# Sturm sweeps as two interleaved chains of 64 steps, and two edits inside the Householder steps, in a two-layer graph network kernel on one core

## The reference, cut to what matters

```
deg    = sum(A, 0) + sum(A, 1) - diagonal(A)
L_norm = d^-1/2 (diag(deg) - A) d^-1/2
_, U   = eigh(L_norm)                       # all 256 eigenvectors
agg    = einsum('mn,bnd->bmd', U.T, h);  o = relu(agg @ W1 + b1) @ W2 + b2
x      = x + einsum('nm,bmd->bnd', U, o)
# second block: two graph convolutions with adj, then LSTMs over windows of 1, 2, 3 and 4 nodes
```

## Time and profile before

| what | us |
|---|---|
| median of three runs | 1768.78 |
| the profiled execution, its own time | 1770.09 |
| span of the profile (first to last instruction) | 1768.2 |
| wide Householder steps (20.0 to 473.8) | 453.8 |
| narrow Householder steps (473.8 to 786.2) | 312.4 |
| first sweep, 64 values (796.4 to 898.8) | 102.4 |
| second sweep, 128 values (912.1 to 1039.4) | 127.3 |
| third sweep, 64 values (1046.1 to 1147.7) | 101.6 |
| everything behind it (1147.7 to 1768.2) | 620.5 |

### The profile page before, as it was taken

The page is one execution under the profiler, slowest core; times in us unless marked ns, Lnnn a source line. Parts: engine busy times, 40 slices in busy tenths (PEclk is TensorE's granted clock), DMA queues, the critical chain, the costliest instruction groups (busy, mean ns, idle before and its releaser), DMA issues.

```text
span 1768.2 us, 25450 instructions
## 1 busy us (share of the span) xinstructions
PE 1292.7 (73%) x5951; PEld 1067.5 (60%) x5951; DVE 1324.6 (75%) x6292; ACT 611.8 (35%) x2145; POOL 391.3 (22%) x2101
## 2 busy tenths in 40 slices
PE   7999999999866677752434323342978999999998
PEld 5777888888745555541222211241757668989897
DVE  7898988888888888888979988897572235555555
ACT  2222222222334442221112111230213367777776
POOL 4333333433455555540000000000000001000000
PEclk9999999999999999997656665575999999999999
DMA  6000000000000000000000000000000000000001
GB/s 156 1 1 1 1 1 1 1 2 1 1 1 1 1 1 1 1 1 0 0 1 0 1 0 1 1 1 1 0 1 1 0 1 1 1 1 25 1 25 48
DMA packets 23403, 12.65 MB, mean 7 GB/s; under 512 B 5075, under 2 KB 22230, under 8 KB 23254
## 3 DMA queue, kind: packets, MB, share of 16 engines
q1 hardware_dynamic: 23254, 11.03, 2.4%
HBM read 6.83 MB, written 4.19 MB: 6 GB/s over the span
## 4 chain that ended last, share of the span: by engine, by line
DVE 49%; PE 31%; issue 9%; POOL 5%; ACT 4%; DVEq 1%; POOLq 0%
PE bank L783 9%; DVE O L982 7%; DVE pa L981 7%; PE bank L785 6%; DVE A L911 4%; PE bank L560 3%; PE bank L563 3%; DVE O L893 2%; DVE junk L863 2%; DVE zc L905 2%; DVE wk L897 2%; PE bank L701 2%; PE bank L728 2%; ACT H L507 2%; DVE NG L878 2%
## 5 line engine op out<-in xcount | busy, mean ns | idle before, releaser
L507 ACT ACTIVATE H<-bank,gate_b 128x128 f32<-128x128 f32 (+2 forms) x624 | 213.5, 438 | 81.9 <-PE bank L785 79.3
L563 PEld LDWEIGHTS bank<-O 128*128 128x128 f32 x764 | 201.5, 344 | 0.0
L783 PE MATMUL bank<-O,WlT 128*128 128x128 f32 (+1 forms) x896 | 191.8, 328 | 7.7 <-DVE O L1244 5.6
L641 PE MATMUL bank<-chg,fold 128*128 128x512 bf16 x64 | 31.4, 544 | 221.9 <-DVE chg L956 221.9
L572 PE MATMUL bank<-O,y 128*128 128x2 f32 x510 | 142.4, 349 | 65.4 <-DVE y L863 59.9
L560 PE MATMUL bank<-ident,O 128*128 128x128 f32 x382 | 148.3, 457 | 46.9 <-DVE O L893 35.6
L394 ACT ACTIVATE ncp<-pc,RC 128x2 f32<-128x2 f32 (+1 forms) x254 | 74.9, 295 | 293.4 <-DVE RC L884 293.4
L572 PEld LDWEIGHTS bank<-O,y 128*128 128x128 f32 x510 | 128.2, 312 | 77.6 <-issue 72.2
L785 PE MATMUL bank<-H,WlT 128*128 128x128 f32 (+2 forms) x768 | 169.1, 301 | 0.0
L783 PEld LDWEIGHTS bank<-O,WlT 128*128 128x128 f32 x896 | 148.0, 192 | 24.6 <-issue 7.3
L563 PE MATMUL bank<-O 128*128 128x1 f32 x764 | 162.8, 305 | 0.0
(11 more groups left out here) (364 smaller groups left out, 2958.5 us busy)
## 6 DMA issues: line engine op xcount, KB each, us to landing
X<-in_x SPq DMA_DIRECT2D x2, 2048.0 KB, 13.4
out<-X SPq DMA_DIRECT2D x32, 128.0 KB, 1.9
adj_sb<-in_adj SPq DMA_DIRECT2D x1, 256.0 KB, 3.0
W1s<-in_L_gnn_W SPq DMA_DIRECT2D x1, 64.0 KB, 10.9
W2s<-in_L_gnn_W SPq DMA_DIRECT2D x1, 64.0 KB, 3.9
Wg0s<-in_L_gnn_Wg SPq DMA_DIRECT2D x1, 64.0 KB, 3.6
Wg1s<-in_L_gnn_Wg SPq DMA_DIRECT2D x1, 64.0 KB, 3.7
Wl<-in_L_gnn_Wih SPq DMA_DIRECT2D x1, 0.5 KB, 6.8
```

The costliest lines, as they stand in the source:

```text
L507: ins = a(gates[:, q, i, 0:n], gate_at(p, q, i), fn, bias=gate_b[:, p - 1, i:i + 1])
L563: ins = mm(bank[0][:, 0:1], R[:, b, k, 0:1].to_broadcast([P, P]), R[:, b, k, 0:1], start=(b == bl[0]), stop=(b == 1))
L783: last = mm(gate_at(p, q, i), WlT[:, 0, p - 1, i, :], window(c, p, t, part), start=True, stop=(t == 0))
```

## The change

In the sweeps each half of the matrix is cut again. Chain A runs the first 64 entries of the half. Chain B runs the next 64 entries, and because it does not know what A will deliver, it carries two solutions u and v at once, as a pair of rows; the result is joined at the end from A's and B's ends. One step of the loop now issues A's product, B's product, A's next polynomial, B's next polynomial. A's operations have w elements, B's have 2w. The loop has 64 steps instead of 128. Signs and changes of both chains are taken in one instruction of double width each 8 steps. Scaling is done twice in a sweep (steps 31 to 36, and 59 to 61 with the end). A correction `corr` joins the counts. The parts `wy(n)` stand one to each 8 steps, the transposes of the weights in the even ones of n = 2 to 16.

In the wide Householder steps VectorE's `half` is gone. TensorE's L563 takes a second column, which holds the unit vector and so delivers the pivot, and ScalarE makes the sign `flip` from it behind the root (now without the factor of 2). In GpSimd's list the waits for yb_ready and c_ready ahead of tm have changed places. Some tiles share memory now.

```
-    NCH = STEPS // CH
+    BLK = STEPS // 2
+    NCH = BLK // CH
...
+                    pool.wait_ge(S["c_ready"], k + 1)
                     pool.wait_ge(S["yb_ready"], k + 1)
-                    pool.wait_ge(S["c_ready"], k + 1)
                     g.tensor_tensor(tm[:, bs], yb[:, bs], RC[:, k, 0:1].to_broadcast([P, w]), ALU.mult).then_inc(S["t_ready"], 1)
...
-                a(root[:], bank[0][:, 0:1], ACT.Sqrt, scale=4.0).then_inc(S["root_ready"], 1)
+                a(root[:], bank[0][:, 0:1], ACT.Sqrt, scale=1.0 if k < P - 1 else 4.0).then_inc(S["root_ready"], 1)
+                if k < P - 1:
+                    a(flip[:], bank[0][:, 1:2], ACT.Sign, scale=-1.0, bias=neg_tiny[:]).then_inc(S["flip_ready"], 1)
...
+                    a(sgn[:, :, o + 1:o + 9, 0:w], rings[:, :, o:o + 8, 0:w], ACT.Sign).then_inc(S["sgn_ready"], 1)
...
+                    if 1 <= n <= 21:
+                        wy(n)
+                    if n % 2 == 0 and 2 <= n <= 16:
...
-                    ins = mm(bank[0][:, 0:1], R[:, b, k, 0:1].to_broadcast([P, P]), R[:, b, k, 0:1], start=(b == bl[0]), stop=(b == 1))
+                    n = 2 if k < P - 1 else 1
+                    ins = mm(bank[0][:, 0:n], R[:, b, k, 0:1].to_broadcast([P, P]), R[:, b, k, 0:n], start=(b == bl[0]), stop=(b == 1))
...
+                if k == 0 or b0:
+                    dve.wait_ge(S["xrow_ready"], k + 1)
+                if b0:
+                    ts(half[:], x0, 0.0, 0.5, ALU.is_lt, ALU.subtract).then_inc(S["half_ready"], 1)
...
+                if b0 == 0:
+                    dve.wait_ge(S["flip_ready"], k + 1)
+                    tt(pb, root[:], flip[:], ALU.mult).then_inc(S["pb_ready"], 1)
...
+                        if k + 1 < P - 1:
+                            dve.wait_ge(S["xrow_ready"], k + 2)
                         dve.wait_ge(S["add0"], k + 1)
...
+                    if j % 8 == 4 and j > 8:
+                        changes(n - 1, w)
+                    if j == 36:
+                        mark(tt(poly[:, 2:4, 0:w], poly[:, 2:4, 0:w], pr[:, 0:1, 0:w].to_broadcast([P, 2, w]), ALU.mult))
...
+                        mark(tt(uv_now, uv_now, pr[:, 1:2, 0:w].unsqueeze(1).to_broadcast([P, 2, 2, w]), ALU.mult))
...
+                    mark(stt(out=pa[:, 0:w], in0=lam[:, 0:w], scalar=dbh[:, j:j + 1], in1=poly[:, ring_a(j), 0:w], op0=ALU.subtract, op1=ALU.mult))
...
+                    mark(stt(out=pb2[:, :, 0:w], in0=lam2, scalar=dbh[:, BLK + j:BLK + j + 1], in1=pair(j, w), op0=ALU.subtract, op1=ALU.mult))
...
+                    mark(stt(out=poly[:, ring_a(j + 1), 0:w], in0=poly[:, ring_a(j - 1), 0:w], scalar=neh[:, j:j + 1], in1=pa[:, 0:w], op0=ALU.mult, op1=ALU.add))
...
+                    ins = stt(out=pair(j + 1, w), in0=pair(j - 1, w), scalar=neh[:, BLK + j:BLK + j + 1], in1=pb2[:, :, 0:w], op0=ALU.mult, op1=ALU.add)
...
+                    if j in (31, 59):
+                        v.tensor_reduce(pm[:, 0, 0:w], poly[:, ra:ra + 2, 0:w].rearrange("p i w -> p w i"), AX.X, ALU.max, apply_absolute_value=True)
+                        if j == 31:
+                            mark(v.tensor_reduce(pm[:, 1, 0:w], uv_now[:, :, 0:w].rearrange("p i w -> p w i"), AX.X, ALU.max, apply_absolute_value=True))
...
+                    elif j in (32, 60):
+                        mark(ts(pm[:, :, 0:w], pm[:, :, 0:w], TINY, None, ALU.max))
...
+                    elif j in (33, 61):
+                        mark(v.reciprocal(pr[:, :, 0:w], pm[:, :, 0:w]))
...
+                tt(x_ab, poly[:, 14:16, 0:w], pr[:, 0:1, 0:w].to_broadcast([P, 2, w]), ALU.mult)
+                link(tt(x_uv, poly[:, 30:34, 0:w], pr[:, 1:2, 0:w].to_broadcast([P, 4, w]), ALU.mult))
+                tt(x_uv[:, 0:2], x_uv[:, 0:2], x_ab[:, 1:2].to_broadcast([P, 2, w]), ALU.mult)
+                link(tt(x_uv[:, 2:4], x_uv[:, 2:4], x_ab[:, 0:1].to_broadcast([P, 2, w]), ALU.mult))
+                tt(ends[:, :, 0:w], x_uv[:, 0:2], x_uv[:, 2:4], ALU.add).then_inc(S["ends_in"], 1)
```

More of the change, by code:

```diff
@@ L103, in gnn_kernel @@
         drow = sb("drow", [P, N]); sq = sb("sq", [P, 2])
-        root = sb("root", [P, 1]); half = sb("half", [P, 1]);
+        root = sb("root", [P, 1]); half = sb("half", [P, 1]); flip = sb("flip", [P, 1]); neg_tiny = sb("neg_tiny", [P, 1])
         NG = sb("NG", [P, N, 2]); RC = sb("RC", [P, N, 2]); sh = sb("sh", [P, N])
@@ L128, in gnn_kernel @@
+        pb2 = RC[:].rearrange("p n j -> p (n j)")[:, 0:2 * PTS].rearrange("p (i w) -> p i w", w=PTS)
+        corr = sb("corr", [P, PTS], BF16)
+        sgn = sb("sgn", [P, 2, CH + 1, PTS], BF16); chg = sb("chg", [P, 2, CH, PTS], BF16)
         shift_sum = sb("shift_sum", [P, PTS + 1])
         R = o_rows[:, 18:22].rearrange("p r n -> p (r n)").rearrange("p (b k j) -> p b k j", b=NB, j=2)
-        poly = o_rows[:, 0:9].rearrange("p r (i w) -> p (r i) w", w=PTS)
-        ind0, ind1 = (o_rows[:, i:i + 2].rearrange("p r n -> p (r n)") for i in (10, 12))
@@ L132, in gnn_kernel @@
-        down = o_rows[:, 14:15].rearrange("p r (i w) -> p (r i) w", w=PTS)
-        mid = o_rows[:, 15:18].rearrange("p r (i w) -> p (r i) w", w=PTS)
-        cnt = sb("cnt", [P, LANES]); lo = sb("lo", [P, LANES]); junk3 = sb("junk3", [P, LANES, 64]); lamj = sb("lamj", [P, 2])
+        poly = o_rows[:, 0:23].rearrange("p r (i w) -> p (r i) w", w=PTS)
+        ind0, ind1 = (m[:].rearrange("p r n -> p (r n)") for m in (below, A))
+        unit_row = ones[:, 0:PTS]
+        rings = poly[:, 0:32].rearrange("p (q i) w -> p q i w", q=2)
@@ L955, in changes, with pair, begin @@
                 o = 8 * (n % 2)
-                tt(chg[:, o:o + 8, 0:w], sgn[:, o + 1:o + 9, 0:w], sgn[:, o:o + 8, 0:w], ALU.mult).then_inc(S["chg_ready"], 1)
+                tt(chg[:, :, o:o + 8, 0:w], sgn[:, :, o + 1:o + 9, 0:w], sgn[:, :, o:o + 8, 0:w], ALU.mult).then_inc(S["chg_ready"], 1)
+            def pair(j, w):
+                return poly[:, ring_u(j):ring_v(j) + 1:ring_v(j) - ring_u(j), 0:w]
+            def begin(w):
+                for row, rows, val in ((14, 1, 0.0), (15, 1, 1.0), (30, 1, 0.0), (31, 2, 1.0), (33, 1, 0.0)):
+                    ins = v.memset(poly[:, row:row + rows, 0:w], val)
+                return mark(ins)
             for s in range(SWEEPS):
```

205 lines of the change are left out of this document (115 added, 90 removed).

## The result

| | before | after |
|---|---|---|
| median time, us (4 runs each) | 1769.45 (1768.65 to 1770.25) | 1697.88 (1696.84 to 1699.08) |
| span of the profiled execution, us | 1768.2 | 1697.1 |
| mean granted clock of TensorE | 0.906 | 0.927 |
| the three sweeps, us | 102.4, 127.3, 101.6 | 76.2, 109.0, 73.1 |
| wide Householder steps, us | 453.8 | 453.5 |

The ratio is 0.9597, with a 95% interval from 0.9585 to 0.9609: 4.0% faster. One of the seven executions of the kernel before that were taken beside e5 to e8 lasted 4553 us, and the ratios leave it out.

What follows compares the result with a forecast made beforehand. VectorE's chain of dependent short operations was taken to bound the sweeps; loops 205.1, changes 16.4, scaling 14.6, holds 13.0 and ends 12.7 made 261.8 against 331.3; 1770.1 - 69.9 + 0.5 = 1700.7 profiled, 1699.4 us median, range 1691 to 1714.

Steps and rivals of the forecast that it cites:

- The loops: 64 steps in each of three sweeps, independent operations issued 0.085 before the previous end: 59.8, 85.5, 59.8, together 205.1 us.
- changes: Sweeps: one double-width changes instruction per 8 steps, 7 inside a loop; 4.2 + 8.0 + 4.2 = 16.4 us.
- Scaling: Two scalings in each sweep (reductions, clip, reciprocal, products): 14.6 us over the three sweeps.
- The ends: End of each sweep (products, corr, one changes, fills in two sweeps): 4.0, 5.5 and 3.2, together 12.7 us.
- GpSimd's holds: Sweeps: GpSimd's 13 instructions hold VectorE as before, 5.5 + 4.5 + 3.0 = 13.0 us.
- rival 3: Sweeps: the squaring chain binds, each of some 14 halves late by 1 us, giving 1713 us; chance 10%.
- rival 1: Sweep loops: no overlap, independent operations follow end to end, 65 us back, giving 1765 us; chance 3%.
- rival 2: Sweep loops: B's pair of rows costs 0.8 ns extra an element, +52, giving 1752 us; chance 5%.
- rival 4: Sweep loops: B's pair of rows costs 2.0 ns extra an element, +131, giving 1831 us, slower than before; chance 2%.
- The Householder steps: Both edits there, all 127 wide steps: +0.5 us in sum, between -3 and +8.
- the sign by ScalarE: First 48 wide Householder steps: without half, VectorE reaches the reductions sooner, 0.00 to 0.07 a step, together -2.4 us.
- the turned waits: Later wide Householder steps: tm starts 0.14 instead of 0.08 after yb, 0.065 a step where that chain decides, +2.9 us.

Runs made afterwards that it cites:

- e5: The changed kernel with one pair of waits turned, pb_ready kept with VectorE's NG and xm_ready ahead, in all 255 Householder steps: 1695.93 us, ratio 0.9581.
- e8: e7 with seven of GpSimd's sums of the squaring with the identity moved to VectorE: 1664.09 us, ratio 0.9403.
- e1: The changed kernel with each loop instruction of the sweeps also waiting for the one right ahead of it: 1792.8 us, ratio 1.0129.
- e6: The changed kernel with GpSimd's operations of the squaring in the sweeps on 4 of 512 columns, the rest left out: 1686.63 us, ratio 0.9527.
- e3: The changed sweeps with the Householder steps of the kernel before (half, old root, old order of GpSimd's waits): 1697.69 us, ratio 0.959.
- e2: The changed kernel with GpSimd's two waits ahead of tm back in their old order: 1693.95 us, ratio 0.957.
- e4: The changed kernel with five pairs of waits in the Householder steps (tm, ym, NG, wk, y) keeping the last-met wait with its instruction: 1670.34 us, ratio 0.9434.
- e7: e4 with a sixth pair of waits turned, root_ready kept with pb in the narrow steps: 1665.39 us, ratio 0.9413.
- e9: The changed kernel with both the edit of e2 (tm's waits) and that of e5 (NG's waits): 1685.76 us, ratio 0.9524.

## Why the prediction was right, point by point

**The loops**: 205.1 forecast. Taking the median distance from one start to the next for each of the four lines, times their number, the loops come to 58.75 + 84.35 + 58.66 = 201.8 us. The distances are 0.196 and 0.263 where the forecast had 0.200 and 0.267: 3.3 us of the 3.5 by which the sweeps were over-priced (261.8 against 258.3). The forecast took 0.285 and 0.352, the lengths of operations that wait, and an overlap of 0.085. Those that don't wait last 0.272 and 0.339 and overlap by 0.076; the two errors nearly cancel. e1 shows that the overlap is the cause.

**changes**: 16.4 forecast, 4.2 + 7.9 + 4.2 = 16.3 found, with 1.21 for 2048 elements where the forecast's line gave 1.23.

**Scaling**: 14.6 forecast, 3.95 + 7.25 + 3.95 = 15.2 found. **The ends**: 12.7 forecast; 5.2, 6.3 and 3.1 found. In the first and in the second lies a hold by GpSimd of about 1 us (L1076 takes 1.30 at 993.25, and the same operation 0.23 in e6), so some 12.5 without them.

**GpSimd's holds**: 13.0 forecast, 12.3 by e6 (the excess over the medians in the loops is 10.5, and the two holds in the ends are 2.1). This term was a guess from the looks of the trace; e6 came within 0.7 of it.

**The other engines** (rival 3): no idle time of VectorE ahead of L985, so the squaring kept up, at granted clocks of 0.62 to 0.80. **Rivals 1, 2 and 4** would have shown in the starts and lengths of the loop's operations, and don't: 0.20 and 0.26 apart, 344 and 473 ns.

**The Householder steps**: +0.5 forecast as -2.4 + 2.9. By e3 and e2 the sign by ScalarE gives -3.7 in the wide steps, mostly in the first 48, where each won 0.067 on average (a typical one went from 3.73 to 3.67) and not the 0.05 that -2.4 stands for; by e2 and after the turned waits cost +3.0, with 0.14 for 0.08 behind yb as forecast, and 0.5 more in the narrow steps, which the forecast had left out. From before to after the wide steps became 0.3 us shorter and the narrow ones 0.3 longer. The late steps were forecast at 3.50 for 3.43 and alternate between 3.50 and 3.54.

**What the sum owes to chance**: between the two profiled executions, the span fell by 71.1 us where 69.4 were forecast. The sweeps were 3.5 us shorter than forecast, the Householder steps 0.5 and the stretches between the sweeps 0.3. Against that, the start ahead of them came 1.7 us later (21.7 for 20.0), the stretch from the Householder steps to the sweeps grew by 0.2 and the rest behind the sweeps by 0.7. So errors of both signs met, and the total missed by 1.7 here and by 1.5 in the median.

The forecast had nothing for the start. The trace shows what lies there, GpSimd's fill of `sgn` and a small VectorE operation beside it, before:

```profile
4.70 1.91 POOL L250 MEMSET sgn<- 128x2176 bf16 x1
...
6.79 0.56 DVE L822 TENSOR_SCALAR pos<-deg 128x2 f32<-128x2 f32 x1
```

and after:

```profile
4.70 3.72 POOL L265 MEMSET sgn<- 128x4352 bf16 x1
...
6.78 1.75 DVE L843 TENSOR_SCALAR pos<-deg 128x2 f32<-128x2 f32 x1
```

The signs of two chains need a tile of twice the size, so the fill takes 1.8 us longer, and `pos` ends only at 8.53, 0.11 behind the fill's end. It looks like the hold that the sweeps show. No run changed the fill alone.

What was clearly not right was found later, in the study: e5's forecast put the last wait of the step on VectorE, and in many steps it was GpSimd's.

## What to carry to other kernels

- On an engine filled by one chain of short dependent operations, a second independent chain woven in pays even if it adds elements: here 0.12 us for each operation that need not wait for its forerunner, 768 times, against three rows of work a step for two. The length of the operations and the start of an independent one in the same trace give the size beforehand.
- Where an instruction waits for two semaphores, write the wait that ends last so that it stays with the instruction itself; turned round it costs 0.065 us a time, and five such pairs in a loop of 255 steps were worth 27.5 us. Try them together: one alone can be hidden by another that stands wrong.

## What the runs showed of the hardware that was not expected

**An instruction of its own for the second wait has a price, and it counts only if that wait ends last.** In all runs the wait written first stayed with the instruction, and the one written last went ahead of it. When the separate one is met last, the start comes 0.14 us behind the event on GpSimd and 0.10 on VectorE; when the other is, 0.08 and 0.035. That is 0.065 to 0.07 a time on both engines (e2, e4, e5, e7, e9).

**GpSimd and VectorE take turns, and VectorE without gaps can keep GpSimd waiting for long.** GpSimd's sums of 512 columns in the changed kernel (start, length):

```profile
854.55 1.54 POOL L337 TENSOR_TENSOR O<-ident,Pm 128x512 f32<-128x512 f32 x1 [18.33 <-ACT Pm L420]
...
912.77 4.54 POOL L337 TENSOR_TENSOR O<-ident,Pm 128x512 f32<-128x512 f32 x1 [39.55 <-ACT Pm L420]
937.15 1.34 POOL L337 TENSOR_TENSOR O<-ident,Pm 128x512 f32<-128x512 f32 x1 [19.84 <-ACT Pm L420]
965.66 4.54 POOL L337 TENSOR_TENSOR O<-ident,Pm 128x512 f32<-128x512 f32 x1 [27.18 <-ACT Pm L420]
...
1027.75 1.30 POOL L340 TENSOR_TENSOR O<-O,ident 128x512 f32<-128x512 f32 x1 [33.27 <-ACT O L420]
```

Where one takes about 1.3, one VectorE operation beside it stretches: L1028 at 1027.85 took 1.28 for 0.27 and ended at 1029.13, with GpSimd's at 1029.05. The two of 4.54 are in the second sweep. There VectorE's operations ran on at their usual lengths from 912.98, through the `changes` instruction at 914.95, and only L1028 at 916.09 was stretched, to 1.37, ending at 917.46 with GpSimd's at 917.31. The Trainium skill, page "SBUF — State Buffer", section "Who interferes with whom", says that the port pair the two share is an exclusive lock, that a VectorE instruction with two inputs in SBUF contends with a GpSimd instruction that reads SBUF, and that the order of issue decides who blocks. The stretch of one operation to the end of the other agrees. The 4.54 is not explained by the order of the recorded starts: GpSimd's instruction was the first by its start (912.77), and yet overlapping VectorE operations that began later (912.98 and on) went ahead for 3.3 us.

Two runs bear on it. In e1, where VectorE leaves 0.036 us between the same operations, all four sums of the second sweep took 1.26 to 1.28. In e6 GpSimd's operation has 4 columns, and the same two places still took 3.45, so it is waiting and not work. The first of them, with the `changes` instruction beside it:

```profile
907.98 3.45 POOL L337 TENSOR_TENSOR O<-ident,Pm 128x4 f32<-128x4 f32 x1 [38.95 <-ACT Pm L422]
...
910.14 1.22 DVE L987 TENSOR_TENSOR chg<-sgn 128x2048 bf16<-128x2048 bf16 x1
```

It ends 0.07 behind the end of `changes` (911.43 and 911.36). The changed kernel and the six others in which both operations have their 512 columns show the same two long turns, and in all of them GpSimd's operation ends 1.12 to 1.16 us behind the end of `changes`. So the turn ended with `changes` each time. Elsewhere GpSimd got its turn among the loop's operations, with no `changes` near (937.15, 1027.75). Why it did not in these two places stays open.
